# The first two groups of queries and keys copied from SBUF to SBUF, head by head, with a shorter run of dummy products before them

## The reference

```python
c6 = jax.nn.silu(c) @ Wc + bc
sh_msa, sc_msa, g_msa, sh_mlp, sc_mlp, g_mlp = jnp.split(c6, 6, axis=-1)
xm = _modulate(_ln(x), sh_msa, sc_msa)
q = (xm @ Wq + bq).reshape(B, S, NH, DH)      # 16 heads of 16
k = (xm @ Wk + bk).reshape(B, S, NH, DH)
v = (xm @ Wv + bv).reshape(B, S, NH, DH)
q = q / DH
w = jnp.einsum('bqhc,bkhc->bhqk', q, k)
w = jax.nn.softmax(w, axis=-1)
y = jnp.einsum('bhqk,bkhc->bqhc', w, v).reshape(B, S, H)
x = x + g_msa[:, None, :] * (y @ Wo + bo)
```

## Time and profile before

| | us |
|---|---|
| median of 3 runs | 929.71 |
| lowest, highest | 926.41, 933.15 |
| the profiled execution | 927.77 |
| its span in the profile | 925.6 |

### The profile page before, as it was taken

One profiled execution on the slowest core, in us unless ns is written; L12 is line 12 of the kernel. 1 busy time (PEld: TensorE's weight loads), 2 busy tenths in 40 slices (PEclk: granted clock), 3 DMA queues, 4 the chain that ended last, 5 costly groups with the idle time before them and its releaser, 6 DMA issues.

```text
span 925.6 us, 14715 instructions
## 1 busy us (share of the span) xinstructions
PE 878.1 (95%) x5294; PEld 539.3 (58%) x5294; DVE 587.9 (64%) x916; ACT 518.9 (56%) x955; POOL 468.7 (51%) x614
## 2 busy tenths in 40 slices
PE   5999999999989999998999999999999999999997
PEld 3453444444347779776878775444444433687874
DVE  4687887788895366554533277878777886234323
ACT  2226878776784444444364441677866778744331
POOL 4393565564748645447544424748255016665330
PEclk9979999999999999999999999999999999999999
DMA  7565584666212030123214136546636531100001
GB/s 231 153 160 163 155 248 121 183 173 186 85 57 91 1 134 1 36 72 139 79 48 180 12 95 173 154 127 184 177 112 200 138 108 58 38 14 1 23 24 45
DMA packets 67087, 101.30 MB, mean 109 GB/s; under 512 B 19644, under 2 KB 30984, under 8 KB 66632
## 3 DMA queue, kind: packets, MB, share of 16 engines
q1 hardware_dynamic: 58584, 86.90, 31.6%
q0 software_dynamic: 5920, 10.90, 4.6%
q10 hardware_dynamic: 2512, 2.58, 1.1%
HBM read 64.65 MB, written 35.02 MB: 108 GB/s over the span
## 4 chain that ended last, share of the span: by engine, by line
PE 78%; DVE 10%; ACT 4%; issue 4%; POOL 3%; DMA 0%; SPq 0%; DVEq 0%; POOLq 0%; ACTq 0%
PE PS L1151 13%; PE PS L715 12%; PE PS L689 12%; PE PS L1133 12%; PE PS L644 5%; PE PS L700 4%; PE PS L625 3%; PE PS L620 3%; DVE U L877 3%; ACT PH L779 2%; PE PS L456 2%; PE PS L657 2%; PE PS L633 1%; PE PS L474 1%; PE PS L1269 1%
## 5 line engine op out<-in xcount | busy, mean ns | idle before, releaser
L877 DVE TENSOR_REDUCE U<-PS 128x2 f32<-128x1024 f32 x256 | 307.8, 1220 | 55.3 <-PE PS L700 53.7
L779 ACT ACTIVATE PH<-PS 128x512 f32<-128x512 f32 x512 | 275.4, 605 | 87.8 <-PE PS L689 84.8
L689 PE MATMUL PS<-UR 50*128 50x512 f32 x512 | 187.4, 456 | 9.3 <-ACT PH L779 4.6
L700 PE MATMUL PS<-UR 48*128 48x512 f32 x512 | 190.9, 469 | 5.4 <-DVE U L877 4.7
L1199 POOL TENSOR_TENSOR PHR<-PH,PHR 128x512 fp32r<-128x512 f32 x96 | 124.1, 1296 | 118.6 <-ACT PHR L1189 118.6
L689 PEld LDWEIGHTS PS<-UR 50*128 50x128 f32 x512 | 79.2, 186 | 147.2 <-ACT PH L779 84.6
L1151 PE MATMUL PS<-UR,PHR 128*128 128x256 f32 x768 | 158.6, 290 | 4.1 <-POOL PHR L1199 4.0
L715 PE MATMUL PS<-PH,U 128*32 128x512 f32 x1024 | 137.2, 608 | 0.3 <-ACT PH L779 0.3
L1151 PEld LDWEIGHTS PS<-UR,PHR 128*128 128x128 f32 x768 | 124.6, 189 | 21.5 <-issue 18.5
L1151 PE MATMUL PS<-W2R,PHR 128*128 128x256 f32 x384 | 108.1, 282 | 0.0
L1188 ACT ACTIVATE PH<-PS,col 128x512 f32<-128x512 f32 x64 | 43.9, 687 | 93.5 <-PE PS L1133 93.5
(11 more groups left out here) (254 smaller groups left out, 1351.2 us busy)
## 6 DMA issues: line engine op xcount, KB each, us to landing
UR<-d_parts SPq DMA_DIRECT2D x112, 192.0 KB, 4.2
d_parts<-UR SPq DMA_DIRECT2D x42, 256.0 KB
d_parts<-UR POOLq DMA_DIRECT2D x40, 256.0 KB, 5.4
d_o<-U SPq DMA_DIRECT2D x32, 256.0 KB, 2.9
U<-in_L_cond_W_dram SPq DMA_DIRECT2D x8, 1024.0 KB, 7.6
W<-in_L_cond_W_dram SPq DMA_DIRECT2D x24, 256.0 KB, 3.3
U<-d_o SPq DMA_DIRECT2D x32, 128.0 KB
U<-d_rec SPq DMA_DIRECT2D x16, 256.0 KB
```

Of the source, the lines that this page charges most:

```text
L689: self.close(pe.matmul(dst, KP[g // 2][r:r + SROWS + 2, j, kt * P:(kt + 1) * P], QP[g // 2][r:r + SROWS + 2, j, :], start=True, stop=True) ...
L700: ins = pe.matmul(bank(2 + (w + 2) % 4), QP[g // 2][r:r + SROWS, j, qt * P:(qt + 1) * P], KP[g // 2][r:r + SROWS, j, :], start=True, stop= ...
L779: nc.scalar.activation(PH[:, m % 2, j, :], self.where("ST", n), ACT.Exp).then_inc(self.a_free, 1)
L877: v.tensor_reduce(mx[:, G % 2, :].rearrange("p (r c) -> p r c", r=2)[:, :, c // 2], PS[:, 2 + (w + 1) % 4:4 + (w + 1) % 4, :], AX.X, ALU.m ...
```

## The change

Groups 0 and 1 of batch 0 are no longer stored and reloaded. A new `fill_first` copies from the split parts to the layout in SBUF, one DMA for each head, slot and kind: 16 partitions of 512 floats. Group 0's queries are issued by SP (12 copies), its keys by ACT (6, `r` = 1) and POOL (6, `r` = 0). Group 1's queries are issued by SP (12) and its keys by POOL (12, counting on `stored[0]`). POOL's stores of the second half stand behind these, without waiting for group 0. Batch 1's split waits for all these copies (`wait_moved`). TensorE's `mod_turn` moves ahead of the dummies, and there are 3 dummies in place of 9. Counters and thresholds follow.

```diff
--- before.py
+++ after.py
@@ -54,6 +54,7 @@
 LEAD, TAIL = -34, NSTEP + 4
 SLOTS = {"Q": (0, 0, 1), "K": (0, 1, 0)}
 FIRST_SLOTS = {"Q": ((0, 1, 0), (0, 2, 1)), "K": ((0, 2, 0), (0, 1, 2))}
+FIRST_FILLED = (18 * 16, 12 * 16, 2 * FILLS, 2 * FILLS)
 SROWS = 48
 SHARED, LAST_SHARED = (7, 0, 1), (7, 0, 1, 4, 5)
 EARLY = ((0, 1, 7), (7, 6))
@@ -672,12 +673,12 @@
             def pe(self, pe):
                 if self.a:
                     pe.wait_ge(mlp1.h_free, FM * B)
+                if self.a == 0:
+                    mod_turn(pe, 2, 3, 6)
                 self.spin(pe, self.spins)
                 for n in self.steps(self.pe_task(pe)):
                     if n == LEAD and self.a:
                         pe.wait_ge(mlp1.acc_free, B)
-                    elif n == LEAD:
-                        mod_turn(pe, 2, 3, 6)
                     if n == 0:
                         pe.wait_ge(self.init, self.a + 1)
                         pe.wait_ge(self.kones, 64 * (self.a + 1))
@@ -693,8 +694,10 @@
                         b, g, r, j, qt = w // 64, w // 16 % 4, 64 - 64 * (w % 2), 2 * (w // 16 % 2) + w // 8 % 2, w // 2 % 4
                         if w % 16 == 0:
                             pe.wait_ge(self.filled[g], self.parts_filled(b, g))
-                            if self.first(b) and g == 1:
-                                pe.wait_ge(first_filled, FILLS)
+                            if self.first(b) and g == 0:
+                                pe.wait_ge(first_filled, 6 * 16)
+                            elif self.first(b) and g == 1:
+                                pe.wait_ge(self.stored[0], 12 * 16)
                         if w % 2 == 0 and w >= 4:
                             pe.wait_ge(self.sm_free, w // 2 - 1)
                         ins = pe.matmul(bank(2 + (w + 2) % 4), QP[g // 2][r:r + SROWS, j, qt * P:(qt + 1) * P],
@@ -721,10 +724,8 @@
                 def task(kind, b, i):
                     if kind == "LNN" and self.a and b < 2:
                         norm_apply(act, "a1", b)
-                    if self.first(b) and (kind, i) == ("WK", 0):
-                        self.save_parts(act, kind, b, i)
-                    elif self.first(b) and (kind, i) == ("FILL", 0):
-                        self.fill(act, b, i, "K")
+                    if self.first(b) and (kind, i) == ("FILL", 0):
+                        self.fill_first(act, 0, "K", self.filled[0], (1,))
                     elif self.first(b) and kind == "MROW":
                         self.maxima(act, b)
                     if not self.on_act(kind) and kind != "O":
@@ -782,7 +783,7 @@
             def split_part(self, eng, link, kind, b, i):
 
                 if b:
-                    eng.wait_ge(*self.parts_saved(i, b - 1))
+                    self.wait_moved(eng, i, b - 1)
                 k = kind == "SK"
                 if self.a:
                     self.wait_read(eng, "R" + kind[1], b, i)
@@ -918,11 +919,12 @@
                         link(pool.tensor_tensor(high, src, czero[:, 0:1].to_broadcast([P, DH * D]), ALU.add))
                         pool.tensor_tensor(WAR[:, b].rearrange("p k n -> p (k n)"), src, high.bitcast(F32),
                                            ALU.subtract).then_inc(w_parts, 1)
+                    elif self.first(b) and (kind, i) == ("FILL", 0):
+                        self.fill_first(pool, 0, "K", first_filled, (0,))
                     elif self.first(b) and (kind, i) == ("FILL", 1):
-                        pool.wait_ge(self.filled[0], self.parts_filled(0, 0))
+                        self.fill_first(pool, 1, "K", self.stored[0])
                         self.save_parts(pool, "WQ", b, 1)
                         self.save_parts(pool, "WK", b, 1)
-                        self.fill(pool, b, i, "K")
                     elif kind == "NORM":
                         pool.wait_ge(self.oloaded[b % 2], 32 * (self.b0 + b // 2 + 1))
                         pool.wait_ge(self.rloaded[b % 2], 16 * (self.b0 + b // 2 + 1))
@@ -963,10 +965,10 @@
             def parts_saved(self, i, b, quarter=1):
 
                 if self.a:
-                    return self.saved[i], 96 * (b + 1) + (128 + 96 * (quarter if b == 0 else 1) if i == 0 else 0)
+                    return self.saved[i], 96 * (b + 1) + (96 * (quarter if b == 0 else 1) if i == 0 else 0)
                 if b:
-                    return self.stored[i], 96 * b + 64 * i
-                return (self.saved[0], 64 * (1 + quarter)) if i == 0 else (self.stored[1], 64)
+                    return self.stored[i], 96 * b + (192, 64)[i]
+                return self.stored[1], 64
 
             def save_parts(self, eng, kind, b, i, quarter=0):
                 k = kind == "WK"
@@ -977,6 +979,26 @@
                         "d h t -> h d t"), parts_d[2 * i + k][p, c, :]).then_inc(
                             (self.stored if self.a == 0 and (b or i) else self.saved)[i], 16)
 
+            def fill_first(self, eng, g, c, done, rows=(0, 1)):
+                k = int(c == "K")
+                eng.wait_ge(self.split[0], k + 1)
+                for slot, part in enumerate(SLOTS[c]):
+                    for r in rows:
+                        for j in range(2):
+                            h = HD * (4 * g + r + 2 * j)
+                            r0 = 64 * r + HD * slot
+                            eng.dma_start((KD if k else QD)[0][r0:r0 + HD, 2 * g + j, :],
+                                          parts_d[k][h:h + HD, part, :]).then_inc(done, 16)
+
+            def wait_moved(self, eng, i, b):
+                if (self.a, i, b) == (0, 0, 0):
+                    eng.wait_ge(first_filled, 6 * 16)
+                    eng.wait_ge(self.stored[0], 12 * 16)
+                    for g in range(2):
+                        eng.wait_ge(self.filled[g], self.parts_filled(0, g))
+                else:
+                    eng.wait_ge(*self.parts_saved(i, b))
+
             def fill(self, eng, b, g, kinds="QK"):
                 eng.wait_ge(*self.parts_saved(g // 2, b, int(b > 0 or g > 0)))
                 if b:
@@ -984,16 +1006,15 @@
                 for c in kinds:
                     k, dst = int(c == "K"), (QD if c == "Q" else KD)[g // 2]
                     src = d_parts[self.a, 4 * b + 2 * (g // 2) + k]
-                    done = first_filled if self.first(b) and (c, g) == ("K", 1) else self.filled[g]
                     for r in range(2):
                         for s0, s1, at_ in FIRST_SLOTS[c] if self.first(b) else ((0, 3, 0),):
                             r0 = 64 * r + HD * at_
                             eng.dma_start(dst[r0:r0 + HD * (s1 - s0), 2 * (g % 2):2 * (g % 2) + 2, :],
                                           src[s0:s1].rearrange("s d h t -> (s d) h t")[
-                                              :, 4 * (g % 2) + r:4 * (g % 2) + 4:2, :]).then_inc(done, 16)
+                                              :, 4 * (g % 2) + r:4 * (g % 2) + 4:2, :]).then_inc(self.filled[g], 16)
 
             def parts_filled(self, b, g):
-                return FILLS * (self.b0 + b + 1) + (FILLS if g != 1 else 0)
+                return FILLS * (self.b0 + b) + FIRST_FILLED[g]
 
             def maxima(self, eng, G):
                 g = G % 4
@@ -1007,13 +1028,15 @@
             def sync_task(self, sp):
                 def task(kind, b, i):
                     if kind in ("WQ", "WK"):
-                        if self.a or (b, kind, i) == (0, "WQ", 0):
+                        if self.a:
                             self.save_parts(sp, kind, b, i)
+                    elif self.first(b) and kind == "FILL" and i < 2:
+                        self.fill_first(sp, i, "Q", self.filled[i])
                     elif kind == "FILL":
-                        if (b, i) == (0, 1):
+                        if (self.a, b, i) == (1, 0, 1):
                             self.save_parts(sp, "WQ", 0, 0, 1)
                             self.save_parts(sp, "WK", 0, 0, 1)
-                        self.fill(sp, b, i, "Q" if self.first(b) and i < 2 else "QK")
+                        self.fill(sp, b, i)
                     elif kind == "MROW" and not self.first(b):
                         self.maxima(sp, b)
                     elif kind == "LDW":
@@ -1809,7 +1832,7 @@
                 sp.wait_ge(out_done, 16 * (B + 1))
 
 
-        att0, att1 = Attention(0, 9), None
+        att0, att1 = Attention(0, 3), None
         mlp0 = MLP(0, "m0", "L0_b1", ACT.Gelu, 0, att0, (W1hA, W2hA, XHA))
         s5 = S5()
         mlp1 = MLP(1, "m1", "L1_b1", ACT.Gelu_apprx_tanh, 1, None, (W1hB, W2hB, XHB))
```

## The result

| | before, us | changed, us | ratio | 95% interval |
|---|---|---|---|---|
| first comparison (9 runs each) | 929.69 | 920.28 | 0.9917 | 0.9888 to 0.9946 |
| again (e1_after_again) | 929.65 | 922.37 | 0.9923 | 0.9888 to 0.9957 |
| again (e9_after_third) | 928.41 | 921.32 | 0.9933 | 0.9901 to 0.9965 |

A ratio is an estimate of its own over the executions in the chip's faster state, not the quotient of the two medians, which would be 0.990 in the first row. The medians differ by 9.4, 7.3 and 7.1 us, where 4.9 was forecast. The first median was inside the forecast range of 920 to 930, at its very edge. The profiled run took 923.69 us for a span of 921.9.

A forecast was written before the change was run, and what follows sets the result against it. The prediction took TensorE's attention stream as the bound, its start waiting for group 0's two trips through DRAM. Gains of 3.7 (copies) and 1.2 (turn) made 4.9, so 929.7 - 4.9 = 924.8 us, range 920 to 930.

The forecast's parts named there:

- Group 0's landing: Start of attention: first queries and keys there at 33.3 (32.9 to 34.6) instead of 37.2.
- issue price of 0.64: Time to issue each small copy on SP and ACT, taken as 0.64 us; on POOL 0.66.
- The slow rival: Copy queues at the start: each copy costs a whole DMA, 1.85 us, giving 936 us; chance 0.05.
- VectorE's 1.2 us: First score reduction: VectorE's lateness of 1.2 us goes away, as the earlier turn lets it unpack modulation columns sooner.
- Group 1 costs nothing: Seventeenth score: group 1, landed by 42.4, is needed at about 45, 42.3 at the earliest, so no cost.
- The sum of 4.9: First score reduction moves from 38.74 to 33.85: 4.9 us gained, bounds 3.6 to 5.2.
- the 3.7 of the copies of group 0: Part of the gain at the first scores: 3.7 us from copying group 0 directly.
- the 1.2 of the turn: Part of the gain at the first reduction: 1.2 us from moving the modulation turn ahead of the dummies.
- the good-way rival: TensorE's clock holds after the first scores: gain 4.9 plus 2 to 3, about 922 us; chance 0.15.
- low stretch of 42 to 49: TensorE in the kernel before, nearly all at 1.2 GHz; holding the clock there would take 3.0 us less.
- idle spot of 1.03 before 40.02: TensorE after the first score pairs, kernel before: idle 1.03 us from VectorE's lateness; said to go away.
- A shift at the start passes through: TensorE, nearly full after the start, carries the start's gain to the end: 4 to 6 us earlier at 100 us.

The follow-up runs named there:

- e1: The changed kernel again with no edit, against the kernel before: 922.37 us, ratio 0.9923.
- e9: The changed kernel a third time with no edit, as yardstick, against the kernel before: 921.32 us, ratio 0.9933.
- e7: The changed kernel with only group 0 copied directly, group 1 going through DRAM as before; ratio 1.0000 to the kernel before.
- e2: The changed kernel with the modulation turn put back behind the three dummies; ratio 0.9956 to the kernel before.
- e5: The kernel before, groups through DRAM, with the turn moved ahead of the dummies and seven dummies; ratio 1.0009 to the kernel before.
- e6: The kernel before, groups through DRAM, with the turn moved ahead of the dummies and three dummies; ratio 1.0000 to the kernel before.
- e12: The changed kernel with SP's twelve group 1 query copies held until POOL's second-half stores landed: 930.68 us, ratio 1.0027 to the kernel before.
- e11: The changed kernel with group 0 stored and reloaded through DRAM, only group 1 copied directly, seven dummies; ratio 0.9998 to the kernel before.
- e4: The changed kernel with no dummies; ratio 0.9941 to the kernel before.
- after: The changed kernel's first profile, from the first comparison with the kernel before; the profiled run took 923.69 us.
- e8: The changed kernel with six of SP's twelve group 1 query copies moved to ACT; ratio 0.9906 to the kernel before.
- e10: Again the changed kernel with six group 1 query copies on ACT, beside the changed kernel: 920.39 us, ratio 0.9921 to the kernel before.

## Why the prediction was right in sign and short in size

- **Group 0's landing: nearly right, and beside the point.** Forecast first scores at 33.3 (32.9 to 34.6), measured 34.47, 32.70 and 33.50. The issue price of 0.64 was 0.62 on ACT and 0.59 by median on SP, where single issues took up to 1.61 (2.91 in e1) while other queues ran, so its 24 took 16.4 to 19.0 us, not 15.4. POOL was cheaper, 0.49 in place of 0.66, so its norm began at 37.24, not near 39.4. Landing, taken as 3.5, had a median of 2.8, up to 6.4. The slow rival, a whole DMA's cost per small copy, did not happen. The Trainium skill's rule ("DMA: Bandwidth & Descriptors", Rules for kernel authors), to coalesce transfers under 64 KB, would have spoken against the change; here 48 copies of 32 KB beat larger stores and reloads, and e7 shows that it is the dependent trip through DRAM that they save.
- **VectorE's 1.2 us: right in place.** It was ready at 33.9 and started 0.6 behind the first scores instead of 1.7 behind. Moving the turn wasn't what did it (e2).
- **"Group 1 costs nothing": the step that failed.** The prediction compared its landing with the seventeenth score, found room, and dropped it. The room was 42.4 against 42.3 to 45, so none at its lower end, and the landing was later than 42.4: SP's last copy, issued at 37.64 in the first profile and 39.69 in e1, took 6.4 and 5.2 us, so group 1 was there at 44.0 and 44.9. The seventeenth score waited 0.35, 2.67 and 2.29. And the same question was never asked of the kernel before. There group 1 landed at 49.3, the seventeenth ran at about 50, and no wait was to be seen, because the clock had slowed the sixteen scores ahead of it to the same time. e5, e6 and e7 uncovered the wait: 2.90 to 3.75.
- **The sum of 4.9 was thus the right order by the wrong term.** The shift is that of the seventeenth score, from about 50.0 to 44.1, 44.9 and 45.3, so 4.7 to 5.9, and 5.6 to 6.7 at the first transposed score. Neither the 3.7 of the copies of group 0 nor the 1.2 of the turn brings anything measurable alone (e5, e6, e7: ratios 1.0009, 1.0000, 1.0000). That the first median fell inside the range was luck as far as the working goes: the two terms of the sum are not what was gained, and the first comparison, 9.4, was the largest of the three.
- **The clock: the good-way rival held in part, by less than it was priced.** Every run has its granted clock, and (1 - clock) x 2 x span is its time at the 1.2 GHz level. Over the 93 runs of the kernel before in the three sets of experiments this was 23.4 us on average, over 30 runs of the changed kernel 20.6, and lines through each kernel's runs rise by 0.26 and 0.35 us for each us of it. That makes 0.7 to 1.0 us of the mean difference of 7.4; the lines' ends at no low time lie 8.4 apart, which a fit over so little range can't pin down. The rest, 6 us and more, is the size of the shift at the first transposed score (5.6 to 6.7). The prediction also put the low stretch of 42 to 49 down to the idle spot of 1.03 before 40.02; that isn't shown, since 1.06 us of idle before 34.47 in the changed kernel were followed by ten microseconds at 1.00.
- **"A shift at the start passes through": right.** e12 shows it for a loss. In the pair of first profiles ACT's first and last copy of an attention output out of PSUM (before and then changed) shows 6.0 us shrinking to 3.8:

```profile
82.51 0.60 ACT L736 ACTIVATE U<-PS 128x512 f32<-128x512 f32 x1 [0.43 <-PE PS L715]
...
794.85 0.58 ACT L736 ACTIVATE U<-PS 128x512 f32<-128x512 f32 x1
```

```profile
76.48 0.60 ACT L737 ACTIVATE U<-PS 128x512 f32<-128x512 f32 x1 [0.43 <-PE PS L718]
...
791.08 0.58 ACT L737 ACTIVATE U<-PS 128x512 f32<-128x512 f32 x1
```

The changed kernel's profile has low stretches where the other was at 1.00:

```profile
261.00:265.00 4.00, 4.00 (x14) 0.57 0.01 2
...
561.00:586.00 25.00, 23.35 (x82) 0.86 0.59 168
```

The kernel before has one of its own at 280 to 285 (0.66), so the one at 561 to 586 is the extra one. They come at other places in other profiles of the same kernel (440 to 450 at 0.83 in e1), so the 2.2 us is most likely one execution's luck, not a cost of the change; one pair of profiles is no measure of a shift this small.

## What to carry to other kernels

An instruction that runs just as its data lands shows no wait, yet it may be held by that landing: when two conditions end together, a trace names neither. Before pricing a faster first step, list when each later group of data lands and when the engine would reach it, in the kernel before too, with the clock at its best; the first one without slack is what the change is worth. Where two paths end together, test each alone and both: here neither alone brought a gain that could be measured (though e11, group 1 alone, had its group 0 later than before), and both brought seven.

## What the runs showed of the hardware that was not expected

- 48 copies of 32 KB between SBUF tiles from three queues: issue 0.48 (POOL), 0.59 (SP), 0.62 us (ACT) by median, landing 1.9 / 2.8 / 6.4 us (min, median, max). SP's issues stretch to 1.61 (2.91 in e1, 2.02 in e9) while POOL's stores of 256 KB run beside them.
- A store and dependent reload through DRAM is dear in time beside other transfers: in e7 from SP's first store of group 1 at 29.28 to the score that uses it at 51.27, 22 us; the direct copies of the same group, issued on SP from about 30, were in use at 44 to 45.
- Runs with 1 us more at the 1.2 GHz level took 0.26 to 0.35 us longer. Half the rate and a TensorE that is 95% busy would suggest 0.5 x 0.95 = 0.48.
- TensorE idle for 3.9 and 2.65 us before the first scores was followed by granted clocks of 0.54 (e4, 34 to 45) and 0.51 (e11, 39 to 53), idle of 3.25 by 0.57 (e7, 35 to 45), of 2.41 and 4.18 by 0.83 (e2, 34 to 44; e6, 38 to 48); with idle of 0.5 to 1.7 us at the same place the first ten microseconds ran at 1.00 in after, e1, e5, e8, e9, e10 and e12.
